# Biases folded into the last row of each weight, and a set-up in another order, in a transformer layer with expert FFNs

## The reference

```
gates = softmax(n @ Wg + bg)            # 8 experts; the top 2 kept, rescaled to sum 1
out   = sum over the top 2 of gate * (n @ We[e] + be[e])
xp = n @ Wp.T + bp ;  q, k, v = xp @ Wq.T + bq, xp @ Wk.T + bk, xp @ Wv.T + bv
attention over the 3 neighbours s-1, s, s+1, 16 heads of 16 ;  attn @ Wo.T + bo
```

## Time and profile before

| | |
|---|---|
| three executions | 1081.43, 1078.80, 1081.26 us (median 1081.26) |
| profiled execution | 1078.79 us, span 1076.9 us |
| PE busy | 1027.7 us, 95% of the span |
| PEld (weight loads) busy | 846.0 us, 79% |
| DVE busy | 863.5 us, 80% |
| ACT busy | 544.0 us, 51% |
| POOL busy | 713.4 us, 66% |
| TensorE clock granted, mean | 0.994 |

### The profile page before, as it was taken

How to read it: one execution, slowest core, us unless ns; L and a number is a source line. 1 busy time by engine, 2 the same in 40 slices (tenths; PEclk the granted TensorE clock), 3 DMA queues, 4 the chain that set the end, 5 groups by cost and what they waited for, 6 DMA issues and landing times.

```text
span 1076.9 us, 17752 instructions
## 1 busy us (share of the span) xinstructions
PE 1027.7 (95%) x5277; PEld 846.0 (79%) x5277; DVE 863.5 (80%) x2405; ACT 544.0 (51%) x1219; POOL 713.4 (66%) x956
## 2 busy tenths in 40 slices
PE   4899999999999999999999999999999999999785
PEld 3687788888888888888888888888888888887563
DVE  3659888988878898888888888888888888888882
ACT  4365555555445555554455555445555554544331
POOL 3375577766667776766777776677777666664453
PEclk9999999999999999999999999999999999999998
DMA  5011000000000000000000000000000000000000
GB/s 171 11 33 36 13 20 20 21 15 7 20 20 21 20 22 11 10 21 20 20 20 21 20 1 21 20 20 21 21 21 1 21 20 20 11 10 11 10 11 20
DMA packets 12615, 23.04 MB, mean 21 GB/s; under 512 B 2244, under 2 KB 5844, under 8 KB 12520
## 3 DMA queue, kind: packets, MB, share of 16 engines
q1 hardware_dynamic: 9240, 13.37, 3.5%
q0 software_dynamic: 3280, 8.53, 2.8%
HBM read 12.46 MB, written 8.39 MB: 19 GB/s over the span
## 4 chain that ended last, share of the span: by engine, by line
PE 86%; DVE 8%; issue 2%; DMA 1%; ACT 1%; SPq 0%; POOL 0%; POOLq 0%; ACTq 0%; DVEq 0%
PE ffn_bank L1007 20%; PE ffn_bank L1009 20%; PE ffn_bank L1008 20%; PE tr_bank L1040 5%; PE mix_bank L1007 4%; PE mix_bank L1009 4%; PE mix_bank L1008 4%; PE tr_bank L1053 3%; PE mix_bank L1085 1%; DMA we_raw<-in_L_ffn_We 1%; PE tr_bank L1007 1%; PE tr_bank L1008 1%; PE tr_bank L1009 1%; DVE chain_sum L737 1%; DVE score L769 1%
## 5 line engine op out<-in xcount | busy, mean ns | idle before, releaser
L1007 PE MATMUL ffn_bank<-we_hi,T_hi 128*128 128x512 f32 x1024 | 409.5, 400 | 4.2 <-DVE chain_sum L737 3.8
L1009 PE MATMUL ffn_bank<-we_hi,T_lo 128*128 128x512 f32 x1024 | 401.0, 392 | 0.0
L1008 PE MATMUL ffn_bank<-we_lo,T_hi 128*128 128x512 f32 x1024 | 400.0, 391 | 0.0
L488 ACT ACTIVATE we_raw<-ffn_bank,gate 128x256 f32<-128x256 f32 x512 | 207.3, 474 | 163.6 <-PE ffn_bank L1009 119.9
L346 POOL TENSOR_TENSOR chain_sum<-chain_sum,we_raw 128x512 f32<-128x512 f32 x128 | 166.2, 1299 | 117.6 <-DVE chain_sum L737 115.0
L1007 PEld LDWEIGHTS ffn_bank<-we_hi,T_hi 128*128 128x128 f32 x1024 | 192.5, 188 | 44.3 <-DVE chain_sum L737 5.5
L1009 PEld LDWEIGHTS ffn_bank<-we_hi,T_lo 128*128 128x128 f32 x1024 | 192.2, 188 | 41.8
L1008 PEld LDWEIGHTS ffn_bank<-we_lo,T_hi 128*128 128x128 f32 x1024 | 192.7, 188 | 35.0
L737 DVE SCALAR_TENSOR_TENSOR chain_sum<-ffn_bank,gate,we_raw 128x256 f32<-128x256 f32 x256 | 111.6, 476 | 54.8 <-ACT we_raw L488 35.1
L737 DVE SCALAR_TENSOR_TENSOR chain_sum<-ffn_bank,gate,chain_sum 128x256 f32<-128x256 f32 x256 | 111.4, 476 | 36.9 <-PE ffn_bank L1009 36.8
L323 POOL TENSOR_TENSOR var_eps<-mean_var,eps 128x2 f32<-128x2 f32 x96 | 28.3, 295 | 152.2 <-DVE mean_var L658 152.2
(11 more groups left out here) (128 smaller groups left out, 1652.1 us busy)
## 6 DMA issues: line engine op xcount, KB each, us to landing
out_x<-y SPq DMA_DIRECT2D x31, 256.0 KB
we_raw<-in_L_ffn_We SPq DMA_DIRECT2D x2, 1024.0 KB, 13.8
x_in<-in_L_attn_x,x_row POOLq DMA_INDIRECT x60
x_in<-in_L_attn_x SPq DMA_DIRECT2D x2, 256.0 KB, 7.6
moved_qk<-qk SPq DMA_DIRECT2D x4, 124.0 KB
w_raw<-in_L_attn_Wq SPq DMA_DIRECT2D x1, 256.0 KB, 2.9
w_raw<-in_L_attn_Wk SPq DMA_DIRECT2D x1, 256.0 KB, 3.1
w_raw<-in_L_attn_Wv SPq DMA_DIRECT2D x1, 256.0 KB, 3.9
```

Of the source, the lines that this page charges most:

```text
L488: last = nc.scalar.activation(scaled[:, f, t, half, j], ffn_bank[b][:, j * D:(j + 1) * D], ACT.Copy, scale=gate[:, 2 * f + t, e:e + 1])
L1007: nc.tensor.matmul(dest, hi[:, t, k, :], w_hi_[:, k, c0:c1], start=(first and k == 0), stop=False, skip_group_check=not first)
L1008: nc.tensor.matmul(dest, hi[:, t, k, :], w_lo_[:, k, c0:c1], start=False, stop=False, skip_group_check=not first)
L1009: last = nc.tensor.matmul(dest, lo[:, t, k, :], w_hi_[:, k, c0:c1], start=False, stop=(k == KB - 1), skip_group_check=not first)
```

## The change

1. **Biases.** Every weight W becomes W[k] - W[last row] in its first 255 rows, and the bias is put in row 255; the normalised rows get 1.0 in column 255, once, at the start. `gate_parts`, `gateT_step`, `bias_step`, `base_step`, `seed_step` and the set-up of the biases are gone. `x_in` has four slots instead of two, and `sum_step` adds the residual itself. A column of Wp is treated in the same way, with bp beside it.
2. **Loads.** SP's queue now issues x of pair 0, be (into one partition), and then We in four parts of 512 columns ("banks"). Each part is three transfers: the last row copied to 128 partitions (`we_last`), rows 0 to 127, and rows 128 to 254, which go to partitions 0 to 126. Then Wp, Wq, Wk, Wv, Wo, and x of pair 1. Wg and bg come over ACT's queue, of which one transfer also has 127 partitions.
3. **Order.** We is corrected and split bank by bank (`we_set_step`, `we_hi_step`, `we_lo_step`), and the set-up of the other weights (`wT_step`, `wo_step`, `wqkv_step`) runs in step -1 beside pair 0.

```diff
-            for w, W in enumerate((Wq, Wk, Wv, Wo, Wp)):
+            sp.dma_start(x_in[:, 0, :, :], x_tiles[:, 0:2, :]).then_inc(x_loaded[0], 16)
+            sp.dma_start(we_raw[PART - 1:PART, 1, :], be.rearrange("(o e) n -> o (e n)", o=1)).then_inc(be_loaded, 16)
+            for b in range(4):
+                at, experts = slice(b * BANK, (b + 1) * BANK), slice(2 * b, 2 * b + 2)
+                sp.dma_start(we_last[:, at].rearrange("p (e n) -> p e n", e=2),
+                             We[experts, LAST, :].partition_broadcast(PART)).then_inc(we_loaded[b], 16)
+                sp.dma_start(we_raw[:, 0, at].rearrange("p (e n) -> p e n", e=2),
+                             We[experts, 0:PART, :].rearrange("e p n -> p e n")).then_inc(we_loaded[b], 16)
+                sp.dma_start(we_raw[0:PART - 1, 1, at].rearrange("p (e n) -> p e n", e=2),
+                             We[experts, PART:LAST, :].rearrange("e p n -> p e n")).then_inc(we_loaded[b], 16)
+            for w, W in ((4, Wp), (0, Wq), (1, Wk), (2, Wv), (3, Wo)):
                 sp.dma_start(w_raw[:, w, :, :], W.rearrange("(k p) n -> p k n", p=PART)).then_inc(
                     w_loaded if w < 4 else wp_loaded, 16)
...
+            def we_set_step(b):
+                at = slice(b * BANK, (b + 1) * BANK)
+                dve.wait_ge(we_loaded[b], 16 * 3)
+                nc.vector.tensor_tensor(we_raw[:, 0, at], we_raw[:, 0, at], we_last[:, at], ALU.subtract)
+                nc.vector.tensor_tensor(we_raw[0:PART - 1, 1, at], we_raw[0:PART - 1, 1, at], we_last[0:PART - 1, at],
+                                        ALU.subtract).then_inc(we_set, 1)
...
+            def wT_step():
+                pe.wait_ge(w_loaded, 16 * 4)
...
+            def wqkv_step(db):
+                if db == 0:
+                    pe.wait_ge(wT_copied, 3)
+                    pe.wait_ge(wp_set, 1)
+                    pe.wait_ge(bp_loaded, 16 * KB)
+                    pe.wait_ge(bqkv_loaded, 16 * 3)
+                else:
+                    pe.wait_ge(wo_lo_done, 1)
...
+            def first_body(s):
+                pe.wait_ge(consts_set, 1)
+                T_step(TA, s + 1, s)
+                logits_step(s)
+                logitsT_step(s)
+                ffn_step(FFN1, s + 1, s + 1, 0, range(0, 2))
+                wT_step()
+                wo_step(s)
+                ffn_step(FFN1, s + 1, s + 1, 0, range(2, 4))
+                wqkv_step(0)
+                wqkv_step(1)
...
-                gateT_step(s)
...
-                    bias_step(FFN2, s)
...
-                if (s + 1).within(PAIRS):
-                    bias_step(FFN1, s)
```

More of the change, by code:

```diff
@@ L371, in _ @@
             rstd_step(LN1, Step(0))
+            for k in range(KB):
+                pool.dma_start(wp[:, k, LAST:D], bp.rearrange("(k p) -> p k", p=PART)[:, k:k + 1]).then_inc(bp_loaded, 16)
+            for w, b_ in enumerate((bq, bk, bv)):
+                pool.dma_start(bqkv_row[:, w * D:(w + 1) * D], b_.rearrange("(o n) -> o n", o=1)).then_inc(bqkv_loaded, 16)
+            pool.dma_start(bo_all[:], bo.partition_broadcast(PART)).then_inc(bo_loaded, 16)
             def gather_step(n, s):
@@ L446, in flat_step @@
                 await_(act, logits_done, g.times(1))
-                nc.scalar.activation(flat_logits[:], flat_bank, ACT.Identity, bias=bg_col[0:NF * 2 * E, 0:1]).then_inc(flat_copied, 1)
+                nc.scalar.copy(flat_logits[:], flat_bank).then_inc(flat_copied, 1)
             def second_step(g, cs):
@@ L1092, in ffn_step @@
                 for b in banks:
+                    if f == FFN1 and n.const == 0 and t == 0:
+                        pe.wait_ge(we_lo_done, b + 1)
                     if t == 1:
@@ L1124, in projection_step @@
                 last.then_inc(proj_done, 1)
-            T_step(TA, Step(0), Step(-1))
-            pe.wait_ge(setup_dve, 2)
-            for bank, c0, c1 in ((mix_bank[0], 0, 2 * D), (mix_bank[1], D, 3 * D)):
-                for mb in range(KB):
-                    last = nc.tensor.matmul(bank[:, :], bp_wide[:, mb, :], wT[:, mb, c0:c1],
-                                            start=(mb == 0), stop=(mb == KB - 1))
-            last.then_inc(setup_pe, 1)
-            pe.wait_ge(setup_dve, 6)
@@ L1137, in _ @@
-            for mb in range(KB):
-                last = nc.tensor.transpose(tr_bank[0][:, mb * PART:(mb + 1) * PART],
-                                           bqkv[:, 2 * D + mb * PART:2 * D + (mb + 1) * PART], ident[:])
-            last.then_inc(setup_pe, 1)
-            pe.wait_ge(setup_act, 9)
-            for mb in range(KB):
-                last = nc.tensor.matmul(mix_bank[0][:, 0:D], bv_wide[:, mb, :], woT[:, mb, :],
-                                        start=(mb == 0), stop=(mb == KB - 1))
@@ L1145, in _ @@
-            last.then_inc(setup_pe, 1)
+            def wT_step():
+                pe.wait_ge(w_loaded, 16 * 4)
+                for w, bank in enumerate((mix_bank[0], mix_bank[1], tr_bank[0])):
+                    for ob in range(KB):
+                        for mb in range(KB):
+                            last = nc.tensor.transpose(bank[:, mb * D + ob * PART:mb * D + (ob + 1) * PART],
+                                                       w_raw[:, w, ob, mb * PART:(mb + 1) * PART], ident[:])
+                last.then_inc(wT_done, 1)
@@ new lines, in wo_step @@
+            def wo_step(s):
+                pe.wait_ge(gate_ops, (s + 1).times(GATE_OPS, 2))
+                for ob in range(KB):
+                    for mb in range(KB):
+                        last = nc.tensor.transpose(tr_bank[1][:, mb * D + ob * PART:mb * D + (ob + 1) * PART],
+                                                   w_raw[:, 3, ob, mb * PART:(mb + 1) * PART], ident[:])
+                last.then_inc(wo_done, 1)
+            def wqkv_step(db):
[4 more added lines that the diff above has]
+                    pe.wait_ge(bqkv_loaded, 16 * 3)
+                else:
+                    pe.wait_ge(wo_lo_done, 1)
+                for dest, c0, c1 in ((mix_bank[db][:, :], 0, 2 * D), (tr_bank[db][:, 0:D], 2 * D, 3 * D)):
+                    for mb in range(KB):
+                        last = nc.tensor.matmul(dest, wp[:, mb, db * PART:(db + 1) * PART], wT[:, mb, c0:c1],
+                                                start=(mb == 0), stop=(mb == KB - 1 and db == 0))
+                    if db == KB - 1:
+                        last = nc.tensor.matmul(dest, last_row[:], bqkv_row[:, c0:c1], start=False, stop=True)
+                last.then_inc(wqkv_done, 1)
@@ L1155, in body @@
                 if s.const == 4:
-                    ffn_step(FFN1, s, s, 0, range(3, 4))
                     projection_step(s - 4, s - 1)
@@ L1215, in fill_body @@
             def fill_body(s):
-                if s.const >= 1:
-                    ffn_step(FFN1, s, s, 0, range(3, 4))
                 if s.const >= 0:
```

367 lines of the change are left out of this document (142 added, 225 removed).

## The result

The changed kernel takes 1085.85 us (median of 6 runs, 1083.87 to 1086.38), the kernel before beside it 1081.35 (1078.8 to 1082.34). The ratio is 1.0042, with a 95% interval of 1.0029 to 1.0055: 4.5 us slower. Beside the experiments it came out at 1.0038 (1.0025 to 1.0052). The forecast was 1091 us in a range of 1079 to 1106. The time lies in the range, but the forecast was a loss of 9.7 us and the measured loss is 4.5. One execution of a later run (1262.8 us, at a mean granted clock of 0.75) is left out of that run's median.

The account below looks back on a forecast made before the run. PE was taken to bound the middle steps, DVE the last ones, and the landing of the weight loads the start. 1078.8 us - 19.9 gained in the steps + 32.7 lost at the start = 1091.6; predicted 1091, range 1079 to 1106.

Parts of the forecast that it names:

- The start: Set-up before pair 0's second tile: 127-partition loads of We go through one DMA engine, Wo lands at 59 us, 32.7 us lost.
- the mark: First product of pair 0's second tile on PE, where the start ends: predicted at 72.5 us, against 39.77 before.
- The middle steps: Steps 4 to 30: one transpose and four bias products leave PE, 0.59 us a step, 15.9 us gained.
- The first steps: Steps 0 to 3: step 0 gains 0.6 us at the scaling, steps 1 to 3 gain 0.35 us each from bias products.
- The last steps: Step 31 gains 0.35 us, steps 32 to 34 nothing as DVE sets the pace, the last step 2.0 us.
- the gate_parts operations: DVE's two small operations in steps 32 to 34, run while PE is still at the projection DVE needs: given nothing.
- The base: Starting time of the sum: the profiled execution of the kernel before, 1078.8 us; its other two executions lie 2.5 us higher.
- The clock: PE in the start: rival that its clock stays low after the wait, 2.8 us more, 1094.4 us, chance 0.03.
- The faster rival: Loads of the start: 127-partition parts are shared out like the others, mark at 34.5, 1053.6 us, chance 0.12.

Follow-up runs that it names:

- the kernel with cut loads: The changed kernel with each of the four 127-partition loads of We's lower half issued as two, of 112 and 15 partitions: 1046.42 us, ratio 0.9687 to the kernel before.

## Why the prediction was half right

- **The start: right in its cause and size, not in every part.** One engine, 24 GB/s, the banks 12.1 us apart, Wo at 57.1 us (59), PE's work from there 13.9 us (13.5), the mark at 71.1 (72.5). By the Trainium skill, DMA: Bandwidth & Descriptors, section "Why a DMA increments its semaphore by 16 and not by 1", 127 partitions go through one engine and 124 through four; the runs agree (0.07 and 24 GB/s; 1054.7 us, with 1054 expected). What the prediction had wrong is that the other fifteen would be done by about 20 us. They carried their shares in bursts between the slow parts (0.81 in the window 50 to 55), since SP's issues stood behind each such part and Wo was only issued at 50.68 us. The sum didn't suffer, because it followed the one engine that all had to wait for.
- **The middle steps: right.** 0.56 us a step, 0.59 predicted; 14.4 us over 26 steps, where 15.3 was predicted.
- **The first steps:** 3.0 us gained where the sum had 0.6 + 3 x 0.35 = 1.65. The excess is in step 0: from the mark to the next double transposes it is 17.8 us before and 16.0 now, so 1.8 gained and not 0.6; the steps behind it gave 0.4 each. In step 0 of the kernel before PE waits 1.51 us for `gate_parts` and 0.35 for gateT, and in the changed kernel only 0.34 us for `normed`. I had let the scaling of the earlier trace rows hold PE in their place; the timeline shows no such wait. No run took this apart.
- **The last steps: wrong, and this is the step that failed.** "In steps 32 to 34 DVE sets the pace [...] so I give them nothing", and of the base additions on POOL "removing them brings nothing". From the last double transposes to the end the sum had 0.59 + 0.35 + 2.0 = 2.9 us, the trace shows 7.1. I had looked at which operations leave DVE, not at what makes those that stay slow. POOL's addition stretched DVE's products by 1.1 us in the steps 32 and 33 (shown by taking it out and by putting it back), and by as much in step 31, where ACT's bias work would have held DVE as long (1.5 us for both and the seeds, 0.35 in the sum). Another 3.3 us, not 2.0, came from the bias path's waits in the steps 34 and 35: I had priced the last step's and overlooked the 1.1 us on PE behind the projection of step 34. The reason given for the gate_parts operations, that PE's projection hides them, was right: put back, they cost nothing. I had written that POOL's missing additions "may free DVE a little in the last steps", and then gave that no number.
- **The base.** The sum was made against the low execution of 1078.8, 2.5 us under the median. Against the median of 1081.35 the same terms (32.7 - 19.9) give 1094.2 us, so it is in part luck that the forecast is no further off. The profiled execution of after took 1085.55 where the sum was 1091.6: of these 6.0 us, 4.2 are the last steps, 1.4 the start and 1.35 the first steps, less 0.9 for the middle ones.
- **The clock.** The Trainium skill, TensorE: Matmul & The Clock Gate, Part 4, has it that transposes don't count as busy in the way products do; the prediction read it so that banks 2 and 3 would run at 1.2 GHz, at 0.43 us a product. Only the first three took 1.39 us (0.46 each), and from 61.89 on products follow each other by 0.23 us, 2.4 GHz. It cost 0.7 us, 0.5 was predicted. Since products stand between the transposes and the rise, this trace alone can't say which brought it; in the kernel before only the sixteen transposes stand ahead of L998 at the faster pace, which speaks against the page.
- **The faster rival** (127 partitions shared out, 1053.6 us, with the mark at 34.5) did not happen, but it is the kernel with cut loads, which came out still faster: mark 31.95, 1046.4 us, 3.1% faster than before and 3.6% faster than the changed kernel.

## What to carry to other kernels

A load over 127 partitions isn't a load over 128 that lacks one: cut it in two that can be shared out (112 and 15), which here turned a change that lost 0.4% into one that gains 3.1%. Before an operation on an idle engine is priced at nothing, look at how long the neighbours' operations take beside it and without it; the same six DVE products took 3.17 and 2.07 us in different steps of the changed kernel, and the trace of the kernel before held a hint, 2.23 us at 110.90 and 2.9 to 3.2 us in all later steps. In the steps where the pipeline drains, each wait between engines has to be looked up by itself, since the one engine that hides everything in the middle has run out of work.

## What the runs showed of the hardware

A one-engine transfer doesn't only make itself late: SP's issue of the next one stood for 9.86 us (in the changed kernel four of its issues took 8.8 to 10.7 us), so that nothing behind it was even handed over, and the fifteen other engines ran out of work. And the granted clock in the windows read 1.00 from 20 to 26 us in the changed kernel while its products of 512 columns followed each other by 0.43 us, the pace of 1.2 GHz:

```profile
24.43 0.63 PE L952 MATMUL ffn_bank<-we_hi,T_hi 128*128 128x512 f32 x1
24.85 0.63 PE L953 MATMUL ffn_bank<-we_lo,T_hi 128*128 128x512 f32 x1
25.28 0.63 PE L954 MATMUL ffn_bank<-we_hi,T_lo 128*128 128x512 f32 x1
```

At the start of this trace the distance between products tells the clock, the column doesn't.
